# A transformer block on eight cores: exchanging two activation buffers, and spreading the bf16 copies of two weight matrices

## The reference, cut to what matters

```python
x = x + _layernorm(_L0_attn_ref(_layernorm(x, axis=-1), L0_attn_Wqkv, L0_attn_Wo), axis=-1)
x = x + _layernorm(_L0_ffn_ref(_layernorm(x, axis=-1), k0, s0, k1, s1, k2, s2), axis=-1)

# _L0_attn_ref, 32 query heads of 128, one key and one value head, ALiBi, causal:
qkv = hidden_states @ Wqkv
scores = jnp.where(causal, einsum(q, k) * scale + alibi, NEG_INF)
return einsum(softmax(scores), v).reshape(B, S, H) @ Wo

# _L0_ffn_ref, three layers with weights of +1 and -1 given as booleans:
h = relu(s0 * (x @ pm1(k0))) * 2.0
h = relu(s1 * (ei(h) @ pm1(k1))) * 2.0
return s2 * (ei(h) @ pm1(k2))       # ei(): the last 20% of the features times -4
```

## Time and profile before

| | us |
|---|---|
| median of 3 runs | 5311.39 |
| lowest and highest run | 5302.34, 5714.11 |
| the profiled execution, whole | 5305.34 |
| its span, from the first to the last instruction of the slowest core | 5303.7 |
| spans of the 8 cores | 5267.9 to 5303.7 |
| TensorE busy (matmuls) | 5100.2 |
| VectorE, ScalarE busy | 1697.2, 1404.5 |
| DMA, mean over the span | 180 GB/s |

### The profile page before, as it was taken

The page is one execution under the profiler, slowest core; times in us unless marked ns, Lnnn a source line. Parts: engine busy times, 40 slices in busy tenths (PEclk is TensorE's granted clock), DMA queues, the critical chain, the costliest instruction groups (busy, mean ns, idle before and its releaser), DMA issues.

```text
span 5303.7 us, 74679 instructions; the slowest of 8 cores (5267.9 to 5303.7 us)
## 1 busy us (share of the span) xinstructions
PE 5100.2 (96%) x28386; PEld 2512.8 (47%) x28386; DVE 1697.2 (32%) x3061; ACT 1404.5 (26%) x3331; POOL 467.1 (9%) x750
## 2 busy tenths in 40 slices
PE   6999989999989999999999999999999999999998
PEld 4544444455434444455554444455555444444443
DVE  3332212344323331233432333123333114343235
ACT  3321112333100111554430011166555101100002
POOL 0000001111110000000000000000000000101111
PEclk9999999999999999999999999999999999999999
DMA  8779999989999756332234666633222346465487
GB/s 178 135 135 194 185 203 200 212 197 195 203 220 252 243 207 223 134 120 104 104 119 152 221 231 222 213 129 105 96 88 96 136 151 235 174 257 191 151 302 292
DMA packets 125056, 955.24 MB, mean 180 GB/s; under 512 B 14819, under 2 KB 14948, under 8 KB 15076
## 3 DMA queue, kind: packets, MB, share of 16 engines
q0 software_dynamic: 101088, 782.29, 53.9%
q1 hardware_dynamic: 23620, 168.18, 8.8%
HBM read 839.26 MB, written 136.31 MB: 184 GB/s over the span
## 4 chain that ended last, share of the span: by engine, by line
PE 85%; DMA 10%; DVE 2%; issue 1%; DVEq 1%; ACT 1%; SPq 0%; ACTq 0%; POOLq 0%
PE pb L584 47%; PE pb L621 28%; PE pb L492 5%; PE pb L521 4%; DMA wst<-k 4%; DMA wst<-wq 2%; DMA xf<-x1sp 2%; DMA out<-xf 1%; PE pb L535 1%; DVEq L800 1%; DMA Vx<-x 1%; PE pb L506 1%; DMA xf<-x 0%; PE pb L572 0%; DVE xf L770 0%
## 5 line engine op out<-in xcount | busy, mean ns | idle before, releaser
L983 ACT ACTIVATE PT<-pb,eb_sb 128x64 bf16<-128x64 f32 (+4 forms) x2720 | 1012.6, 438 | 1035.6 <-PE pb L521 512.1
L584 PE MATMUL pb<-Ub,wst 128*128 128x512 bf16 x4096 | 1004.6, 379 | 0.0
L584 PE MATMUL pb<-Xb,wst 128*128 128x512 bf16 x4192 | 935.4, 379 | 28.6 <-DMA wst<-wq 22.3
L621 PE MATMUL pb<-wst,Vx 128*128 128x512 bf16 x4096 | 898.5, 382 | 30.3 <-DVE wst L684 28.0
L621 PE MATMUL pb<-wst,Qb 128*128 128x512 bf16 x4096 | 901.8, 382 | 7.9 <-DMA wst<-wob 5.8
L684 DVE TENSOR_SCALAR wst<-wst 128x4096 bf16<-128x4096 bf16 x416 | 518.7, 1248 | 878.6 <-DMA wst<-k 878.5
L584 PE MATMUL pb<-Vx,wst 128*128 128x512 bf16 x3072 | 746.6, 380 | 1.3 <-DVE Qb L807 1.3
L621 PEld LDWEIGHTS pb<-wst,Vx 128*128 128x128 bf16 x4096 | 401.5, 98 | 519.8 <-issue 49.7
L584 PEld LDWEIGHTS pb<-Xb,wst 128*128 128x128 bf16 x4192 | 404.2, 98 | 492.5 <-issue 36.4
L621 PEld LDWEIGHTS pb<-wst,Qb 128*128 128x128 bf16 x4096 | 400.8, 98 | 486.2 <-issue 19.9
L584 PEld LDWEIGHTS pb<-Ub,wst 128*128 128x128 bf16 x4096 | 395.7, 98 | 374.9 <-issue 2.2
(11 more groups left out here) (74 smaller groups left out, 1830.3 us busy)
## 6 DMA issues: line engine op xcount, KB each, us to landing
wst<-k POOLq DMA_DIRECT2D x416, 1024.0 KB, 5.4
wst<-wob POOLq DMA_DIRECT2D x96, 1024.0 KB, 5.2
wst<-wq POOLq DMA_DIRECT2D x68, 1024.0 KB, 13.6
wst<-wqb POOLq DMA_DIRECT2D x68, 1024.0 KB, 6.3
xf<-x SPq DMA_DIRECT2D x56, 1024.0 KB, 10.5
wqb<-wq POOLq DMA_DIRECT2D x34, 1024.0 KB, 19.4
wst<-wo POOLq DMA_DIRECT2D x32, 1024.0 KB, 13.0
x1sp<-xf SPq DMA_DIRECT2D x32, 1024.0 KB, 7.2
```

Source lines behind the costliest of these rows:

```text
L584: m = t.matmul(pb[b][:, :], w[:, c * 128:(c + 1) * 128], fm(src, c), start=(c == 0), stop=(c == 31))
L621: m = t.matmul(pb[b][:, :], src[:, c * TB + tl * 128: c * TB + tl * 128 + 128], w[:, ii * 512:(ii + 1) * 512], start=(c == 0), stop=(c == 31))
L983: m = s.activation(PT[:, g % 4, off:off + w], pb[S0 + g % 2][:, off:off + w], AF.Exp, bias=eb[:, col:col + 1], scale=SCALE)
```

## The change

1. *Buffers.* `LN_DST` is exchanged: ln0 writes `Vx`, ln1 writes `Xb`. The first rows of x, which lay in `Ub` and `Vx`, lie in `Ub` and `Xb`.
2. *Order of the row work.* In wo 1 and wo 2, ln0 now comes ahead of ln2, in `XUSE` and in VectorE's sides. The transposes of ln0 stand in slots 5, 9, 13 and 17. What is left of the sides at the end of a wo stage is done after that stage's last statistics. In qkv 2 and qkv 3 the transposes of ln1 stand in slots 9, 15, 21 and 27 and ScalarE's rstd of the rows of wo comes after tile 3, not tile 0.
3. *Copies.* The 66 copies are spread over the feed-forward stages of blocks 0 and 1: 66 in 190 weight tiles, not 66 in 96. The 32 of Wo fall beside block 0, and 33 of the 34 of Wqkv beside block 1. Wqkv's have a semaphore of their own, `sCvq`, awaited before qkv 3.
4. *Who reads the copy of Wqkv.* Only qkv 3. Qkv 2 loads float32, as qkv 0 and qkv 1 do.

```diff
@@ XUSE
 for _st in ORDER:
+    for _k, _i in LN_AT.get(_st, []):
+        XUSE += [(_k, _i, tl) for tl in range(4)]
     if _st in LN2_AT:
         XUSE += [(2, LN2_AT[_st], tl) for tl in range(4)]
-    for _k, _i in LN_AT.get(_st, []):
-        XUSE += [(_k, _i, tl) for tl in range(4)]
@@ t_slots
     if stage in LN2_AT:
-        return [15 + 5 * tl for tl in range(4)], [13 + 5 * tl for tl in range(4)]
+        return [5 + 4 * tl for tl in range(4)], [3 + 4 * tl for tl in range(4)]
+    if stage[0] == "qkv" and stage[1] > 1:
+        return [9 + 6 * tl for tl in range(4)], [7 + 6 * tl for tl in range(4)]
     return [6 + 6 * tl for tl in range(4)], [4 + 6 * tl for tl in range(4)]
@@ buffers
-    LN_DST = {0: Xb, 1: Vx}
+    LN_DST = {0: Vx, 1: Xb}
@@ GpSimd
                     if stage == ("wo", 1):
-                        gp.wait_ge(sCvt, 16 * 66)
+                        gp.wait_ge(sCvt, 16 * 32)
+                    if stage == ("qkv", 3):
+                        gp.wait_ge(sCvq, 16 * 34)
...
-                            src = (wq_h if i < 2 else wqb_h)[QKV_ORDER[p]]
+                            src = (wq_h if i < 3 else wqb_h)[QKV_ORDER[p]]
...
-                        if kind in LAYER and i == 0:
+                        if kind in LAYER and i < 2:
                             nf += 1
-                            if ncvt < nf * 66 // 96:
+                            if ncvt < nf * 66 // 190:
...
                                     gp.dma_start(out=wqb_h[ncvt - 32],
                                                  in_=wq_h[ncvt - 32]
-                                                 ).then_inc(sCvt, 16)
+                                                 ).then_inc(sCvq, 16)
@@ SyncE (and the same names in row_stats, normalise and first_kv)
-                        sy.dma_start(out=rows32(Ub, Vx, tl)[:, hf * 2048:(hf + 1) * 2048],
+                        sy.dma_start(out=rows32(Ub, Xb, tl)[:, hf * 2048:(hf + 1) * 2048],
@@ TensorE
-                        feature_major(stage, Xb, att_due(0) if i == 0 else NO_ATT, 0, 0, 33)
+                        feature_major(stage, Vx, att_due(0) if i == 0 else NO_ATT, 0, 0, 33)
@@ VectorE
-                            for _ in ln1(i - 1):
-                                pass
+                            for side in rest + [ln1(i - 1)]:
+                                for _ in side:
+                                    pass
...
-                        sides = []
+                        sides = [ln0(li) if k == 0 else ln1(li)
+                                 for k, li in LN_AT.get(stage, [])]
                         if stage in LN2_AT:
                             sides.append(ln2(LN2_AT[stage]))
-                        for k, li in LN_AT.get(stage, []):
-                            sides.append(ln0(li) if k == 0 else ln1(li))
...
-                        for side in sides:
-                            for _ in side:
-                                pass
+                        if kind == "wo":
+                            rest = sides
+                        else:
+                            for side in sides:
+                                for _ in side:
+                                    pass
@@ ScalarE
-                            if p == 0 and i > 0:
+                            if i > 0 and p == (3 if i > 1 else 0):
                                 rstd(("y", i - 1), mvy[:, :, 1], rsy[:, :])
```

More of the change, by code:

```diff
@@ L304, in build_program @@
     sCvt = sem("sCvt")
+    sCvq = sem("sCvq")
     sAff = sem("sAff")
@@ L552, in first_kv @@
                         for c in range(32):
-                            xs = Xb[:, c * TB + tl * 128:c * TB + tl * 128 + 128]
+                            xs = Vx[:, c * TB + tl * 128:c * TB + tl * 128 + 128]
                             wc = w[:, c * 128:(c + 1) * 128]
@@ L691, in row_stats @@
                     L = 4 * LNI[kind, i] + tl
-                    rows = rows32(Ub, Vx, tl) if L < 4 else xf
+                    rows = rows32(Ub, Xb, tl) if L < 4 else xf
                     for j in range(8):
@@ L705, in normalise @@
                     if L < 4:
-                        rows, dst = rows32(Ub, Vx, tl), tm(Qb, tl, 0, D)
+                        rows, dst = rows32(Ub, Xb, tl), tm(Qb, tl, 0, D)
                     else:
```

## The result

| | before | after |
|---|---|---|
| executions (us) | 5302.34, 5311.39, 5556.27, 5714.11 | 5253.52, 5253.91, 5653.46, 6195.47 |
| median of these | 5433.83 | 5453.68 |
| profiled execution | 5305.34 | 5253.52 |
| span of the slowest core | 5303.7 | 5251.9 |
| spans of the 8 cores | 5267.9 to 5303.7 | 5238.8 to 5251.9 |

The ratio of after to before is 0.990, 95% interval 0.9857 to 0.9942: one per cent faster, and "within 2%".

A forecast was written before the change was run, and what follows sets the result against it. TensorE was busy 5100.2 of 5303.7 us, so the change could move only the 203.5 us lost between matmuls and a little clock. Terms -15 - 24 + 4 - 18 - 14 + 25 = -42; 5305.3 - 42 + 2 = 5265, range 5236 to 5303.

The forecast's parts named there:

- f3 0 by the count of DMA time: f3 of block 0: 11 copies instead of 22, 179 us of DMA in 221, no longer DMA-bound; gain 24 us.
- the chain through `xf`: wo of blocks 1 and 2: layer norm 0 goes first, not behind the residual in the one buffer; gains 18 and 14.
- taking the like stage as the measure: qkv of block 2 reads float32 like qkv of block 1, so it loses that stage's 25.0 us.
- I forecast a fast median and add 2.: Whole kernel: 2 us added to the profiled 5305.3, as the median of the runs was 5311.4, 6 above it.
- Copies, block 0, f1 and f2: f1 and f2 of block 0: 22 copies instead of 44 shrink waits towards block 1's; gain 15 us, bounds 0 to 21.
- Its reason, demand: f1 and f2 of block 0: DMA demand falls to 357 of some 555 us, share 0.64, and the queue drains between copies.
- by symmetry a loss: f1, f2 and f3 of block 1 receive 33 copies: about 3 us lost in f1 and f2, 1 in f3.
- A: Rival, 15%: block 0's 46.5 us go by number of copies, half moves to block 1, none is saved; 5300 us.
- B: Rival, 17%: float32 stalls of qkv 1 were inherited from wo 0, so qkv 2 loses only 7; 5247 us.
- C: Rival, 6%: four tiles are too few for layer norm 0, pauses move to slots 9, 13 and 17; 5297 us.
- D: Rival, 7%: in qkv 2 layer norm 1 shares saturated DMA and its transposes wait, slower than before; 5317 us.
- the rate that the prediction set against this term: qkv of block 2: at about 358 GB/s a core, 88 MB take 246 us, so float32 loses 3, not 25; sum 5243.

The follow-up runs named there:

- e9_late: The kernel before, all 66 copies beside block 0, with VectorE's +-1 of a byte tile moved behind the eviction, one tile step later; 5274.04 us.
- e10_pairs: The changed kernel with its 66 copies issued in pairs behind every sixth tile, the same DMA demand in larger pieces; profiled 5289.08 us.
- e3_fp32: The kernel before with float32 Wqkv in qkv 2 and nothing else changed; profiled 5332.25 and again 5335.3 us.

## Why the prediction was right or wrong

| term | predicted | measured, slowest cores | measured, mean of cores |
|---|---|---|---|
| f1+f2 0 | -15 | -28 | -20.8 |
| f3 0, with the wait for Wo's first tile | -29.8 | -29.9 | -29.1 |
| wo 1, the rest | -12.2 | -14.6 | -12.5 |
| wo 2 | -14 | -14.5 | -14.6 |
| qkv 2 | +25 | +27.9 | +26.7 |
| f1, f2, f3 of block 1 | +4 | -0.6 | -0.7 |
| end of the program | 0 | +5.5 | +5.4 |
| whole | -42 | -51.8 | -43.6 |

"Slowest cores" sets core 5 before beside core 7 after; the rest of each whole lies in the other stages.

Right, and by their own reasons: f3 0 by the count of DMA time (share 0.81 forecast, 0.72 found, no wait of TensorE for a byte tile left); both wo stages by the chain through `xf`, with the times of `zn` within 3 us; qkv 2 by taking the like stage as the measure. The profiled execution, 5253.5, against 5265, lies in the range of 5236 to 5303, and a change within 2% was the likeliest case. That the sum, -42, lies so near the mean of the cores, -43.6, is luck: block 0's f1 and f2 gained 6 us more than forecast and block 1 lost 5 less, and the end of the program, qkv 2 and the stages outside the sum took 9 back.

Wrong, step by step:

- *"I forecast a fast median and add 2."* This term of the sum was mis-sized. The median over all executions is 5453.68, which is 200 us above the profiled execution and 150 above the range. In the kernel before, the same term is 5433.83 - 5305.34 = 128. It stands in both columns, so nothing says that it is the change's doing; its cause stays open.
- *"Copies, block 0, f1 and f2 ... I take 15, nearest to block 1's row."* The term came to 28 on the slowest core, above its own bound of 21, and to 20.8 in the mean. The bound took 4.7 us of idle time as what such a stage keeps, from block 1's. But two stages with different attention cannot be compared so: block 1's keeps pauses of its own (4.3 us after), block 0's almost none (0.6, where 5 to 8 was forecast). Of the 28 us, 20 had shown as idle time; the other 8 had been TensorE's busy time, 550.14 us against 541.65, at a granted clock of 0.99 against 1.00.
- *Its reason, demand.* The share fell as computed (0.64 forecast, 0.59 found) but was not the cause: e9_late cured the stage at 0.93 and e10_pairs spoiled it at 0.58. The prediction had named the right one, "a late byte tile also holds up the masks queued behind it"; the price was then taken from the wrong one.
- *"Block 1 ... by symmetry a loss of ... about 3 ... 1 in f3."* 15 - 10 is 5 and not 3, and the loss was nothing. Copies apart by three tiles cost nothing in either block, so there was no symmetry to carry over.
- *What was not in the sum:* 5.5 us at the end of the program (which the prediction put at nothing by not naming it), and the slowest core. Its waits for late tiles and `zn` were larger than the others'; with them gone, the spread of the cores shrank from 36 to 13 us, and the slowest gained 8 us more than the mean.

The rivals. A (copies cost the same wherever they lie) is refuted by f3 1 at 223.3 with ten copies. B (qkv 2 loses only 7) is refuted by 26.7, and by the 25.1 of e3_fp32, where the neighbours are as before. Its sum took too little for a float32 tile, 3.0 us beyond one of 1 MB. The share of the stage is 0.61 with none, 0.88 with 18 and 0.94 with 22 (slowest cores), so 0.015 a tile or 3.6 us, and 34 would ask for 1.12 of 242 us, some 271, where the rival had 250. C and D did not come: `zn` is never waited for in wo 1, wo 2 or qkv 2.

On the rate that the prediction set against this term: in qkv 2 of the changed kernel the window holds 30 float32 tiles of 2.1 MB, 8.4 MB of x, 8.4 MB of x1, three byte tiles of 0.5 and one copy of 3.1 (2.1 read, 1 written), which is 84.4 MB in DRAM in 270.15 us, 312 GB/s at a DMA share of 1.01. (The 199 GB/s of the profile row count each load by what it writes, 1 MB for a float32 tile.) The Trainium skill's page "HBM Reference", section "Specifications (TRN2)", gives about 358 GB/s for each of two cores that stream together. This trace does not reach that, in a stage that wanted all it could get; its traffic is a mixture of converting loads, plain loads and stores, and what a plain stream would reach no run here shows.

## What to carry to other kernels

A queue that serves a stream with a deadline is to be judged in two ways: by demand over the stage where every consumer waits for that stream alone, and by how late a single delivery can come where an in-order engine waits for it with other work behind; pairs of copies cost 26 us beside f1 and f2 of block 0 and at most 0.4 beside the other feed-forward stages. Space the background transfers evenly, and let the in-order engine take the delivery as late as it can; in f1 and f2 of block 0 that one moved instruction was worth as much as halving the copies. And find where the data already lies in the wanted form: a 1 MB store from the weight buffer replaced a 2.1 MB read and a 1 MB write, and freed a later stage.

## What the runs showed that I had not expected

- GpSimd's closing drain takes 3.65 to 3.9 us where all copies lie beside block 0 and 8.55 to 8.7 us where some lie beside block 1, on all cores in all fourteen traces, though the last copy lies over 2000 us back.
- Up to 22 float32 tiles in qkv 2 (a DMA share of 0.94) are free and each one beyond costs 2.2 us; there is no gentle slope before. At 26 tiles 8.8 us were lost at a share that was still 0.93 to 0.95.
- Pairs of copies at a share of 0.58 cost 26 us in f1+f2 0. Twice as many copies, most of them one by one, cost 21 us at a share of 0.92.
